# Mask products of the scores over all 128 rows of TensorE's array instead of two side by side on 64 rows each

## What is computed

```
q, k, v = x @ Wq + bq, x @ Wk + bk, x @ Wv + bv        # 16, 2 and 2 heads of 64
scores[s, w] = q[s] . k[s - 128 + w],  w = 0..255       # 8 query heads share a k head
out = softmax(scores) @ v[window];  attn = out @ Wo + bo
x = layernorm(x + attn)
xr, xk = mu_r * x + (1 - mu_r) * x_prev, mu_k * x + (1 - mu_k) * x_prev
x = layernorm(x + sigmoid(xr @ W_r) * (square(relu(xk @ W_k)) @ W_v))
```

## Time and profile before

| | |
|---|---|
| median of 3 runs | 510.87 us (510.54 to 511.59) |
| time of the profiled execution | 509.77 us |
| its span, slowest core (5) | 508.2 us |
| spans of the 8 cores | 504.9 to 508.2 us |
| PE busy | 440.9 us, 87% of the span |
| ACT / DVE busy | 333.3 us (66%) / 316.5 us (62%) |

### The profile page before, as it was taken

The page is one execution under the profiler, slowest core; times in us unless marked ns, Lnnn a source line. Parts: engine busy times, 40 slices in busy tenths (PEclk is TensorE's granted clock), DMA queues, the critical chain, the costliest instruction groups (busy, mean ns, idle before and its releaser), DMA issues.

```text
span 508.2 us, 10503 instructions; the slowest of 8 cores (504.9 to 508.2 us)
## 1 busy us (share of the span) xinstructions
PE 440.9 (87%) x3052; PEld 220.6 (43%) x3052; DVE 316.5 (62%) x793; ACT 333.3 (66%) x847; POOL 109.0 (21%) x298
## 2 busy tenths in 40 slices
PE   0779999999899869798898988998979988999990
PEld 0344444444444345444363353353435345464640
DVE  0056765654655587576967877877776896545421
ACT  1267868686768575776679496669658769446542
POOL 4330124130403030101122230121123032130303
PEclk9996999999999878899999999999989999999996
DMA  8999429939263646100265286567254548303112
GB/s 108 164 164 195 62 44 115 161 64 140 28 110 54 113 73 117 40 5 1 66 139 135 52 100 156 110 84 187 53 115 115 135 53 177 90 1 103 43 42 83
DMA packets 71448, 48.25 MB, mean 95 GB/s; under 512 B 59104, under 2 KB 60256, under 8 KB 71392
## 3 DMA queue, kind: packets, MB, share of 16 engines
q0 software_dynamic: 11632, 24.88, 28.1%
q1 hardware_dynamic: 59760, 22.70, 22.7%
HBM read 40.85 MB, written 8.39 MB: 97 GB/s over the span
## 4 chain that ended last, share of the span: by engine, by line
PE 59%; ACT 15%; DVE 9%; issue 8%; DMA 5%; POOL 1%; ACTq 0%; SPq 0%; DVEq 0%; POOLq 0%
PE pm L289 11%; PE pm L276 8%; PE pm L319 8%; PE pm L309 6%; PE pm L301 6%; PE po L344 6%; ACT p L383 5%; PE psc L231 4%; DVE nmax L529 4%; PE pm L255 3%; DMA bufq<-wq 2%; PE pm L291 2%; ACT junk L464 2%; DMA yT<-qy 2%; PE pm L270 1%
## 5 line engine op out<-in xcount | busy, mean ns | idle before, releaser
L383 ACT ACTIVATE p<-psc,nmax 128x320 bf16<-128x320 f32 x264 | 138.8, 540 | 96.1 <-DVE nmax L529 95.9
L529 DVE TENSOR_REDUCE nmax<-psc 128x2 f32<-128x640 f32 x132 | 108.1, 821 | 88.8 <-PE psc L237 88.2
L289 PE MATMUL pm<-w16o,ao 128*128 128x512 bf16 x272 | 66.3, 388 | 2.5 <-ACT ao L441 1.2
L541 DVE TENSOR_SCALAR p<-p,rall 128x320 bf16<-128x320 bf16 x264 | 62.4, 299 | 7.6 <-DVE rall L534 0.7
L276 PE MATMUL pm<-bufx,bufq 128*128 128x512 bf16 (+2 forms) x320 | 65.1, 350 | 1.7 <-DMA bufq<-wq 1.7
L301 PE MATMUL pm<-bufx,w16kf 128*128 128x256 bf16 x512 | 62.4, 278 | 2.1 <-ACT pt L397 1.5
L309 PE MATMUL pm<-w16r,bufx 128*128 128x512 bf16 x256 | 59.6, 379 | 5.0 <-DVE zx L565 2.2
L319 PE MATMUL pm<-w16vf,bufq 128*128 128x512 bf16 x256 | 59.5, 380 | 1.8 <-ACT pt L397 1.8
L383 ACT ACTIVATION_READ_ACCUMULATOR p<-psc,nmax 128x1 f32 x264 | 57.1, 216 | 0.0
L301 PEld LDWEIGHTS pm<-bufx,w16kf 128*128 128x128 bf16 x512 | 48.7, 99 | 14.1 <-issue 8.0
L231 PE MATMUL psc<-k,qy 64*128 64x320 bf16 x264 | 41.7, 313 | 13.5 <-ACT p L383 13.1
(11 more groups left out here) (80 smaller groups left out, 572.4 us busy)
## 6 DMA issues: line engine op xcount, KB each, us to landing
zx<-xres POOLq DMA_DIRECT2D x17, 512.0 KB, 6.3
out<-zb SPq DMA_DIRECT2D x16, 512.0 KB, 3.2
bufx<-xt POOLq DMA_DIRECT2D x16, 256.0 KB, 8.9
bufq<-wq POOLq DMA_DIRECT2D x4, 512.0 KB, 10.0
w16o<-wo POOLq DMA_DIRECT2D x8, 256.0 KB, 11.8
w16kf<-wkf POOLq DMA_DIRECT2D x8, 256.0 KB, 5.8
w16r<-wr POOLq DMA_DIRECT2D x8, 256.0 KB, 6.1
w16vf<-wvf POOLq DMA_DIRECT2D x8, 256.0 KB, 6.5
```

Of the source, the lines that this page charges most:

```text
L289: e.matmul(pm[:, bank, :], ao[:, a % 2, kc, :], w16o[:, kc, 512 * b:512 * b + 512], start=(kc == 0), stop=False)
L383: a = e.activation(p16[:, b % 2, j // 2, g, j % 2, :], psc[:, 2 * (n % 2) + g, 0:320], AF.Exp, bias=nmax[:, n % 4, g:g + 1], accum_out=sal ...
L529: e.tensor_reduce(nmax[:, n % 4, :], psc[:, 2 * (n % 2):2 * (n % 2) + 2, 0:320], mybir.AxisListType.X, ALU.max, negate=True).then_inc(s_mx, 1)
L541: t = e.tensor_scalar(part, part, rall[:, b % 2, r:r + 1], None, ALU.mult)
```

## The change

Both mask products of a step are taken over all 128 rows: `rows64` whole as the weights, `mask` whole as what is streamed. Each result is the sum of two equal halves, so that a forbidden key gets -2e30 where it had -1e30, and an allowed one 0 as before. The products of queries and keys (L231) stay on 64 rows each. The number and order of the instructions is the same on every engine; a blank line above moves all later lines of the source by one.

```diff
             for g in range(2):
                 edges = psc[:, 2 * (n % 2) + g, 0:320].rearrange("p (c w) -> p c w", w=64)[:, 0:5:4, :]
-                mm = e.matmul(edges, rows64[64 * g:64 * g + 64, :], mask[64 * g:64 * g + 64, :, :],
-                              start=False, stop=True)
+                mm = e.matmul(edges, rows64, mask[:, :, :], start=False, stop=True)
             mm.then_inc(s_qk, 1)
```

## The result

The changed kernel takes 514.77 us (median of 4 runs, 513.34 to 515.89) where the kernel before takes 510.71 (4 runs). The ratio is 1.0079, with a 95% interval of 1.0046 to 1.0111: about 4 us slower. Forecast were 516.9 us and a range of 513.2 to 520.5. A second set of runs on another chip gave 515.41 against 511.31, ratio 1.0078 (1.0054 to 1.0103). In a few executions the cores of one die ran at a lower clock and took up to a tenth longer; these are left out of every number here.

The account below looks back on a forecast made before the run. Bound mostly by TensorE's queue, with loops through other engines between; 3.6 us of TensorE's time plus 2.4 us of VectorE's later release, 6.0 us on the 510.87 median, gave 516.9 us, range 513.2 to 520.5.

Parts of the forecast that it names:

- the mechanism: TensorE, score steps: change of rows moves ahead of the mask products, which run successively; 0.057 us longer, VectorE released 0.149 later.
- the serial loads: Second mask product waits for the first's end and its own load, 0.317 instead of 0.07: 537 us; chance 0.02.
- The rival without a change of rows: Score to first mask product stays under 0.19 us; 0.093 loss vanishes: -0.4 us, 510.5 us; chance 0.08.
- All six marks: Profile after: intervals 0.23, 0.06 to 0.07, 0.057; score to unit 0.36; maxima about 0.15 later; PE count 3052.
- the 0.093: Microseconds lost on TensorE at the change of rows, behind the mask pair before, in front of the mask products after.
- The term for TensorE's own time: 64 chain steps through TensorE: 58 before long products at 0.057 us, 6 before transposes at 0.044, together 3.6 us.
- part of it is given back: Rival: VectorE's delays meet existing waits, only TensorE's 3.6 us or less stay: 513 to 514.5 us; chance 0.15.
- The term for VectorE: Later release for the maxima, 0.149 us at 16 of 17 steps where the chain leaves for VectorE: 2.4 us.
- 2 us either way: Clock allowance: stretches at TensorE's lower clock could add or take 2 us, since they hardly show in the span.
- the partial cases: Outcomes where waits absorb VectorE's delays and only TensorE's 3.6 us or less stay: 513 to 515 us, chance 0.15.

Follow-up runs that it names:

- the cost was added alone: Kernel before plus a 128 x 128 product on 160 columns ahead of the first unit behind each score step, VectorE released as before: mean span +0.7 us.
- The pair with the 33 products: Kernel before and changed kernel, both with 33 useless products in TensorE's idle gaps: 5.1 us apart (4.6 to 5.6); before with them 3.15 us faster, mean spans.
- the late signal: Kernel before with the signal to VectorE moved onto the first product of the unit behind the mask pair, in 93 of 132 steps: +5.1 us.

## Why the prediction was right, and where it was off

**Right: the mechanism and its sign.** The loss at the change of rows moved, it didn't vanish: 0.24 us in front of the mask products, none behind. The two products run one behind the other, the loads beside them (0.067 apart, not 0.317, so the serial loads are out). The rival without a change of rows wanted under 0.19 and is out. All six marks that the forecast named came as named, but for sizes.

**The prices were a little low.** 0.067 instead of 0.057 us a step on TensorE: I took the 0.013 us that the interval from score to mask pair holds beyond the streaming to be part of the 0.093. It stays and is added. For the same reason VectorE's release is 0.16 later, not 0.149. By the forecast's counts that is 0.9 us on the sum.

**The term for TensorE's own time was too large, and this is the step that failed.** The 58 x 0.057 + 6 x 0.044 = 3.6 us rest on counting steps on the chain of work. The chain follows one path, and a step on it costs its full price only if no wait behind it can shrink. Where the cost was added alone, the ten segments paid for 29 of 43 counted steps; over all 132 the mean span rose by 0.7 us only, net of what the clock gave back. The rival "part of it is given back" looked for this in VectorE's delays, which is the wrong place: of these, most are paid.

**The term for VectorE was right in mechanism and size, and mostly in place.** 16 x 0.149 = 2.4 us were forecast for the exits to the maxima, and the change at 17 steps that the chain names costs 2.4 (1.7 to 3.2). That number contains these steps' share of TensorE's time too, so it is no proof to the tenth. The chain names places less well than a total: steps 102 and 126 cost nothing, and steps that it doesn't name pay in 80 to 88 and 120 to 128, already at the change's own 0.16. That the late signal cost 5.1 and not 3.0 us fits this, for it delays 93 steps, by 0.32 us at the median and so by twice the change's dose, and its time at the lower level grew from 36.6 to 39.7 us a core. How the 5.1 divides between the two is open.

**The clock.** I gave it 2 us either way, without a direction, because core 2 and core 7 of the earlier trace rows did not order by it. It has one: more work on TensorE gave less time at the lower level, and about 1 us came back that way. The whole spans of cores of one execution hide it, since they also start up to 1.2 us apart; their segments, as steps 112 to 120 above, don't.

Together: 6.9 us by counts at the measured prices. Of these the ten segments should hold 43 x 0.067 + 8 x 0.16 = 4.2 us and paid 3.5, and the other 56 steps should hold the other 2.7. The pair with the 33 products shows those apart: with each segment taken from the cores that stayed at the upper level in it (3 to 8 of them), the change costs 2.3 us in the 56 and 3.5 in the ten, 5.8 in all, in single executions. So the counts were about 1.1 us too high, in both parts, and 1.7 came back by the clock; by the mean spans it is 1.8 and 1.0. Which of the chain's links made it count steps that don't pay is open.

That 516.9 came as near to 514.8 as it did is in part luck. The prices were 0.9 us too low and the counts about 1.1 too high, so that the two errors nearly cancelled, and what is left between 6.0 and 4.1 is about what the clock gave back, to which the forecast gave no direction. The range held because it reached down to the partial cases.

## What to carry to other kernels

Products side by side on halves of the rows are worth their 0.06 us a pair, and a change between 64 and 128 rows costs about 0.09 wherever it stands, so moving it wins nothing. Price a change to a busy engine's queue twice, by its own time and by how late it signals: here the change at the 17 steps where the chain leaves for VectorE cost 2.4 us of 4.1, and 0.079 us of engine time alone at 127 steps cost 0.7, net of the clock. And look for stretches at the lower clock and for waits of the matrix engine ahead of them, here of 0.8 to 2.5 us: 33 useless products there won 3.15 us on balance, and nine more, which came behind a wait instead of in it, took nearly all of that back.

## What the runs showed of the hardware that I had not expected

- 33 products of 128 x 128 on 512 columns with no use (7.1 us of TensorE's time at 0.216 each) made the kernel 3.15 us faster in the mean span and 0.37% in the measured time, with the time at 1.2 GHz down from 36.6 to 14.6 us a core.
- The same wait is not always followed by the lower level. In before all eight cores have a wait of 1.8 us near 293 us, and on five of them a stretch at 1.2 GHz follows or has just begun; with one of 2.55 us near 372 it is seven of eight, with one of 1.6 us near 236 none.
- Nine more of them, meant for a wait of 2.55 us, cost 2.4 us in their segment: they first had to wait for ScalarE's release of the bank (`s_ao`), and then ran for the most part at the lower level, for 3.0 to 3.9 us instead of 1.9. I had counted the gap as free.
- The same product is followed after 0.056 us in a run and after 0.067 when it is the first behind a change of rows: 0.01 us that is paid once at each change.
